# First layer's heads: turns of unit s-2 issued before the scores of unit s, and low parts before the maximum

## The reference, cut to what matters

```python
q = jnp.einsum('bsh,he->bse', x, w_q).reshape(b, sq, GROUPS, HPG, KVC)
kv = jnp.einsum('bsh,he->bse', x, w_kv)
k, v = jnp.split(kv, 2, axis=-1)
scores = jnp.einsum('bqgpd,bkgd->bgqpk', q, k) * (SCALE / LAYER_INDEX)
scores = jnp.where(causal[None, None, :, None, :], scores, -jnp.inf)
probs = jax.nn.softmax(scores, axis=-1).astype(x.dtype)
ctx = jnp.einsum('bgqpk,bkgd->bqgpd', probs, v).reshape(b, sq, HEADS * KVC)
return jnp.einsum('bse,eh->bsh', ctx, w_dense)
```

## Time and profile before

| | |
|---|---|
| median of 3 runs | 3699.46 us (3696.17 to 3703.63) |
| profiled execution: time, span | 3702.74 us, 3701.0 us |
| PE busy | 3382.4 us, 91% of the span |
| PEld | 2610.0 us, 71% |
| DVE | 2417.9 us, 65% |
| ACT | 1571.7 us, 42% |
| POOL | 1181.8 us, 32% |
| the stage of the heads | about 75 to 913 us |

### The profile page before, as it was taken

How to read it: one execution, slowest core, us unless ns; L and a number is a source line. 1 busy time by engine, 2 the same in 40 slices (tenths; PEclk the granted TensorE clock), 3 DMA queues, 4 the chain that set the end, 5 groups by cost and what they waited for, 6 DMA issues and landing times. The chain is left out here.

```text
span 3701.0 us, 65212 instructions
## 1 busy us (share of the span) xinstructions
PE 3382.4 (91%) x21360; PEld 2610.0 (71%) x21360; DVE 2417.9 (65%) x4492; ACT 1571.7 (42%) x2875; POOL 1181.8 (32%) x854
## 2 busy tenths in 40 slices
PE   8999999999897999999985779999779999799997
PEld 6888888887666888888862435555368887488883
DVE  4666666666335565656555878887478887488873
ACT  4555555554334444444432326666233333333332
POOL 4011020200225666666642300000114445444444
PEclk9999999999998999999998879999879999899998
DMA  5000000010001000000000412221044442244431
GB/s 175 4 13 16 2 25 3 26 36 1 0 0 51 18 19 17 18 18 17 18 0 23 183 57 81 81 82 65 27 136 109 117 116 71 54 114 110 113 97 49
DMA packets 134112, 199.97 MB, mean 54 GB/s; under 512 B 23120, under 2 KB 78288, under 8 KB 133968
## 3 DMA queue, kind: packets, MB, share of 16 engines
q1 hardware_dynamic: 127888, 190.55, 16.6%
q0 software_dynamic: 6144, 8.39, 1.4%
HBM read 162.06 MB, written 36.57 MB: 54 GB/s over the span
## 5 line engine op out<-in xcount | busy, mean ns | idle before, releaser
L2118 DVE TENSOR_REDUCE l2h_half<-l2h_s 128x1 f32<-128x512 f32 x512 | 337.4, 686 | 50.2 <-PE l2h_s L2020 49.3
L2105 ACT ACTIVATE l2h_PT<-l2h_s 128x1024 f32<-128x1024 f32 x256 | 248.4, 1022 | 164.1 <-PE l2h_s L2030 164.0
L791 DVE TENSOR_REDUCE l0h_negtop<-l0h_sc 128x1 f32<-128x128 f32 (+7 forms) x256 | 193.1, 754 | 187.1 <-PE l0h_sc L687 183.5
L813 DVE TENSOR_TENSOR l0h_PTL<-l0h_tp,l0h_PTH 128x512 fp32r<-128x512 f32 (+3 forms) x384 | 200.6, 550 | 125.3 <-ACT l0h_PTH L869 122.5
L869 ACT ACTIVATE l0h_PTH<-l0h_tp 128x512 fp32r<-128x512 f32 (+3 forms) x384 | 175.4, 496 | 220.3 <-PE l0h_tp L698 220.1
L2020 PE MATMUL l2h_s<-l2h_K,l2h_Q 128*128 128x512 f32 x512 | 217.9, 462 | 23.9 <-DMA l2h_K<-l_split 20.5
L879 ACT ACTIVATE l0h_probs<-l0h_sc,l0h_negtop 128x128 f32<-128x128 f32 (+7 forms) x256 | 190.7, 745 | 115.5 <-DVE l0h_negtop L791 114.5
L159 POOL TENSOR_TENSOR XN<-XN,n_rstd 128x512 f32<-128x512 f32 x24 | 29.9, 1268 | 570.0 <-DVE n_rstd L140 570.0
L765 POOL TENSOR_TENSOR l0a_wq_lo<-l0a_wq,l0a_wq_hi 128x256 fp32r<-128x256 f32 x15 | 11.1, 739 | 608.8 <-ACT l0a_wq_hi L853 608.8
L713 PE MATMUL l0h_cx<-l0h_PTH,l0a_VH 128*128 128x256 f32 (+1 forms) x640 | 183.2, 286 | 17.2 <-DVE l0h_PTL L813 17.2
L698 PE MATMUL l0h_tp<-ident,l0h_probs 128*128 128x128 f32 x1152 | 177.5, 276 | 20.8 <-DVE l0h_PTL L813 20.8
(11 more groups left out here) (449 smaller groups left out, 9911.7 us busy)
## 6 DMA issues: line engine op xcount, KB each, us to landing
l3p_decb<-l_decays SPq DMA_DIRECT2D x128, 256.0 KB, 4.4
l3p_w<-L_w SPq DMA_DIRECT2D x34, 512.0 KB, 3.6
l2h_Q<-l_split SPq DMA_DIRECT2D x64, 256.0 KB
l2h_K<-l_split SPq DMA_DIRECT2D x64, 256.0 KB
l3p_prow<-l_decays SPq DMA_DIRECT2D x128, 128.0 KB, 3.1
l_split<-l2q_hi SPq DMA_DIRECT2D x16, 512.0 KB, 4.0
l_split<-l2q_lo SPq DMA_DIRECT2D x16, 512.0 KB, 3.8
l3p_wgu<-L_ffn_w_gate_up SPq DMA_DIRECT2D x32, 256.0 KB, 4.8
```

Source lines behind the costliest of these rows:

```text
L791: dve.reduce_max(negtop[:, i % 4:i % 4 + 1], sc[s % 2][:, 0:(t + 1) * P], AX_X, negate=True).then_inc(top_ready, 1)
L813: dve.tensor_tensor(PTL[part], tp[n % 2][:, 0:m * P].rearrange("p (m n) -> p m n", m=m), PTH[part].bitcast(F32), ALU.subtract).then_inc(pt ...
L2105: act.activation(PT[:, b, kb, :], s2[kb % 2][:, :], ACT.Exp, scale=L2_SCALE).then_inc(exped, 1)
L2118: dve.reduce_max(half[:, b, t, z:z + 1], bank(slot_of(i))[:, :], AX_X).then_inc(s1_read, 1)
```

## The change

On PE the turns of the unit of s-2 are issued before the scores (or the projection) of slot s instead of after them. On DVE the reciprocal and the low part of the unit of s-2 are issued before the maximum of slot s instead of after it. ACT, SP and POOL are as before, and so are all waits and buffers.

```diff
@@ -729,6 +729,8 @@
                     mm.then_inc(dense_done, 1)
 
                 def step(h, s):
+                    if u := unit_at(h, s, 2):
+                        turn_probs(*u)
                     if exists(h):
                         kind, i = SLOTS[s]
                         if kind == "unit":
@@ -737,8 +739,6 @@
                         elif exists(h + 1 - i):
                             bank_free(h, s)
                             project(h + 1 - i, i, sc[s % 2])
-                    if u := unit_at(h, s, 2):
-                        turn_probs(*u)
                     if (u := unit_at(h, s, 4)) and u[1] % 2:
                         dense(*u)
                     if (u := unit_at(h, s, 3)) and u[1] % 2:
@@ -827,12 +827,12 @@
 
                 def step(h, s):
                     kind, i = SLOTS[s]
-                    if kind == "unit" and exists(h):
-                        row_max(h, s, i)
                     if u := unit_at(h, s, 2):
                         if u[1] % 2:
                             invert(*u)
                         low_probs(*u)
+                    if kind == "unit" and exists(h):
+                        row_max(h, s, i)
                     if kind == "query" and exists(h) and exists(h + 1 - i):
                         low_queries(2 * h + (3 if i == 0 else 2), i, sc[s % 2])
                     if (u := unit_at(h, s, 4)) and u[1] % 2:
```

## The result

| | before | changed |
|---|---|---|
| median | 3698.11 us (4 runs, 3696.17 to 3703.63) | 3720.53 us (4 runs, 3716.19 to 3724.53) |
| ratio, 95% interval | | 1.0050 (1.0034 to 1.0065) |
| profiled execution: time, span | 3702.74, 3701.0 us | 3716.19, 3714.4 us |
| period of a head (weight splits) | 52.22 us | 53.32 us |
| first transpose behind the heads (L754) | 913.2 us | 932.4 us |

The account below looks back on a forecast made before the run. The first layer's heads were taken as bound by PE's own work plus small waits. Per head 2 x (2.11 - 1.6) + 0.31 = +1.33 us, over 15.5 heads +20.6, on 3699.5 gave 3720 us, range 3700 to 3740.

Parts of the forecast that it names:

- Both old waits: PE's waits for DVE's low parts, at turns and at the weighing of values, would go: 1.6 us a batch.
- W(6,7): PE's weighing of values for query tiles 6 and 7; its old wait, counted as 0.75 us, would go.
- T(t4)b: PE's turns of query tile 4, second bank; old wait of 0.74 us before the fifth transpose, a new one about 0.4.
- The chain from S(t4) to T(t5) and on to T(t0): From scores of query tile 4 through DVE and ACT: turns of tile 5 at 6.33 us, of tile 0 at 8.75.
- the split's 0.31 us: ACT's split of query weights, in each head's first batch, would lengthen the new chain by 0.31 us a head.
- PE's own work: PE's work without waits was taken as unchanged; 4.68 us of it runs from scores of tile 4 to turns of tile 5.
- The term that I set to 0: Cost of PE going directly from a dense or weighing to a transpose: bounded by 0 and 0.1 us, taken as 0.
- The size of the waits: New PE waits at turns of query tiles 4, 5 and 0: 1.65 + 0.46 = 2.11 us a batch.
- The sum a head: New waits less old ones in two batches, plus the weight split: +1.33 us a head, period 53.4 to 53.6 us.
- Rival 1: Faster: the chain of ACT and DVE is covered and no new waits come, 3649 to 3667 us; chance 0.11.
- Rival 2: No change: new waits as large as the old replace them, within 7 us of 3699; chance 0.10.
- Rival 3: New waits take PE's clock down to 1.2 GHz for stretches, up to 150 us more, 3850 us; chance 0.02.

Follow-up runs that it names:

- e4: Kernel before, with DVE's low part of query tile 7 put ahead of the maximum of tile 2, PE's order unchanged: 3688.53 us, ratio 0.9961.
- e10: Kernel before, with the dense of query tiles 6 and 7 moved behind the scores of tile 0, its addition behind that tile's maximum: ratio 0.9950.
- e5: Changed kernel, but in the slots of query tiles 0 and 1 PE keeps scores ahead of turns: ratio 1.0076 to the kernel before.
- e3: Changed kernel, with ACT's split of the next head's query weights moved from the slot of query tile 5 to that of tile 3: ratio 1.0040.
- e8: Kernel before, with ACT's split of the query weights moved from the slot of query tile 5 to that of tile 3: ratio 0.9999.
- e7: As e4, and PE also turns query tile 6 ahead of the projection instead of behind it: ratio 0.9970 to the kernel before.
- e1: Kernel before with only PE's half of the change, turns ahead of scores; DVE keeps the maximum first: 3747.78 us, ratio 1.0124.
- e6: As e5, and PE keeps scores ahead of turns in the slot of query tile 6 too: ratio 1.0026 to the kernel before.
- e2: Kernel before with only DVE's half of the change, low part ahead of maximum; PE keeps scores first: 3759.17 us, ratio 1.0150.

## Why the prediction was right

- What goes. Both old waits went, as predicted, and their size holds. e4 gives 0.75 us for W(6,7), as counted. e10 gives 0.57 and the 0.2 to 0.3 that came back, about 0.8, for T(t4)b, where the prediction has 0.74; its count has a slip, for at 0.11 us each the four transposes end at 619.03 and not at 619.07, and the wait is 0.78.
- The chain from S(t4) to T(t5) and on to T(t0): up to T(t5) every start lies within 0.02 us of the prediction, behind it within 0.06, the split's 0.31 us included. e5 shows that it goes on to T(t0), e3 and e8 that ACT's time is in it.
- PE's own work. The prediction left it as it was, 26.04 - 1.6 = 24.44 us a batch (26.04 us is the shorter of the two batches of a head before), 6.64 of it beside the chain, so 17.80 from T(t0) to the next S(t4); the rows have 625.86 - 608.05 = 17.81. This fit is in part luck. The same work in the kernel before, read from its rows, is 26.04 less 6.66 (D(6,7) to D(2,3), 615.80 to 622.46), 0.85 (D(2,3)) and 0.85 (the waits of W(6,7) and T(t7)), which is 17.68 us. So the prediction had 0.1 us too much there and missed 0.1 us a batch by which the work became slower, 4 us over the stage.
- What became slower. The term that I set to 0 was a dense directly ahead of a transpose, and 0 is right: in e7 a dense stands between transposes and takes 0.86 us (621.73 to 622.59), as before (0.85). What I had not listed is a dense directly behind scores: 0.92 us (599.28 to 600.20). The 0.05 us are in its first matmul, which holds PE for 0.272 us behind scores (median of 113 in the changed kernel) and for 0.219 behind transposes (115 before). All four denses of a batch now stand so, two of them outside the chain. Added up by the starts of all matmuls of twelve heads, gaps beyond the usual one taken as waits, PE's own work is some 48.8 us a head before, 49.3 changed and 49.3 in e1, its waits 3.4, 4.0 and 5.8 us: an estimate. Part of the slower work lies beside the chain, where it costs nothing and only makes the visible wait smaller: up to the end of W(2,3) PE needs 604.53 - 599.28 = 5.25 us (604.53 is 604.24 plus 0.29 for the last three matmuls of W), less 0.37 of wait, 4.88 against 4.68 predicted.
- The size of the waits. Predicted 2.11 us a batch; counted 0.37 at the second bank of T(t4) (five transposes take 0.92 us instead of 0.55), 1.06 at T(t5) (605.59 - 604.53), 0.2 each at the dense and T(t0): 1.83. So the idle time ahead of L698 grew to 45.1 us, not to 50 to 70. The sum did not suffer, because it counted the chain and not the waits.
- The sum a head: predicted +1.33, measured +1.10, and the period, 53.32 us, lies just below the 53.4 to 53.6 that were to show it. Without the split a batch has 625.86 - 599.28 = 26.58 us, predicted 26.55; with it 53.32 - 26.58 = 26.74, predicted 26.86. The 0.14 us by which the second batch was longer before (52.22 - 26.04 = 26.18), at the boundary of the loop, now lies in the chain's shadow, and I had kept it.
- The total. Over the stage it is 19.2 us, predicted 20.6, and 0.7 of the 19.2 are the clock's (below). That the median came out at 3720.53 us with 3720 forecast is luck: the medians differ by 22.4 us, 3 more than the stage explains, and the four changed runs lie near 3716 and 3724.
- The rivals. Rival 1 (faster, the chain covered) fell by its own condition: it needed a chain of 4.7 us, and the chain has 6.31. Rival 2 (no change) is outside the interval of the ratio. Rival 3, the clock, did occur in both profiles of the changed kernel, once each, in the last batch of the stage, and cost 0.7 us there; in three relatives it came inside the loop (below). It was no reason for the slowdown, since the fourteen periods of both profiles are free of it, but its chance was set on thin ground.

What stays open: why the clock falls in one head and not in the next (last section), and which other neighbours make up the rest of the slower work of PE (some 0.26 us a batch by the estimate above, 0.21 of it the four denses).

## What to carry to other kernels

Before an engine's step is put ahead of another, follow the queued instructions around one whole ring, engine by engine, at the place where the largest pieces meet: here a reorder that removed 1.6 us of waits a batch made a new chain over DVE and ACT, longer than PE's own work beside it. Change only the slots whose wait the trace shows, look at what the moved instruction now holds back, and move independent work (here a dense product) into the wait that remains. To tell a chain from a busy engine, take a small piece of work out of the supposed chain and the same piece out of the other version: only where it is in a chain does the period move.

## What the hardware showed that I had not expected

In e5 four of the fourteen periods are 1.3 us longer. In one of them, behind the waits at T(t5) and the dense, 512-column matmuls start 0.42 us apart instead of 0.23. Stretches ahead of it, in it, and the same place in an ordinary head (columns as in rows 1; PEclk is the third figure from the end):

```profile
311.00:315.00 4.00, 2.74 (x21) 2.18 (x20) 1.26 (x5) 2.88 (x9) 0.73 (x1) 1.00 0.08 21
315.00:318.40 3.40, 3.40 (x9) 2.63 (x10) 2.43 (x6) 1.30 (x5) 0.00 (x0) 0.50 0.05 13
637.00:641.00 4.00, 2.74 (x18) 1.98 (x16) 1.56 (x5) 2.85 (x10) 0.72 (x1) 1.00 0.12 33
```

The granted clock was 1.2 GHz for 3.4 us and the head 54.6 us long; 325 us later PE was as little busy (2.74 of 4.00 us) and kept 2.4 GHz. The waits ahead of the fall were 0.82 us and 0.28 us, and those of the ordinary head (at 638.97 and 640.13) are the same:

```profile
313.70 0.88 PE L699 MATMUL l0h_tp<-ident,l0h_probs 128*128 128x128 f32 x6 [0.82 <-DVE l0h_PTL L816]
314.86 1.96 PE L728 MATMUL l0h_outp<-l0a_wd,l0h_ctxT 128*128 x4 [0.28 <-ACT l0h_ctxT L892]
```

The four falls stand in successive heads, at 315.0, 369.6, 424.2 and 478.9 us. Two heads of e2 and two of e6 are 1.6 us longer, with the same 3.4 us at 1.2 GHz. The changed kernel, with waits of 0.9 and 1.3 us at T(t5), had none in 28 periods, nor had before and the faster kernels in theirs. But in the last batch of the stage, behind a wait of 1.52 us, the changed kernel fell in both profiles; this is the first, and then the same place of e3, with the same wait and no fall:

```profile
924.40:927.80 3.40, 3.40 (x13) 2.82 (x14) 1.33 (x5) 0.87 (x2) 0.00 (x0) 0.50 0.00 0
```
```profile
924.35 1.47 PE L698 MATMUL l0h_tp<-ident,l0h_probs 128*128 128x128 f32 x6 [1.52 <-DVE l0h_PTL L813]
```
```profile
921.14 0.85 PE L699 MATMUL l0h_tp<-ident,l0h_probs 128*128 128x128 f32 x6 [1.52 <-DVE l0h_PTL L816]
```

From here to the first transpose behind the heads it takes 932.4 - 924.35 = 8.0 us there and 928.45 - 921.14 = 7.3 us in e3, so this fall cost 0.7 us.

The Trainium skill ("TensorE: Matmul & The Clock Gate", section "HAM oscillation — how this bites in real kernels") says that idle gaps between groups of matmuls can take the clock down again and again. The traces agree in kind: every fall inside the loop of e5 came behind such gaps. They add that gaps of a microsecond and less can be enough, and that the gaps alone do not decide, since equal ones went with a fall in four heads of e5 and without one in ten. What decides is not shown. For these kernels a wait of PE cost its length and, in some heads, 1.3 to 1.6 us more.
